# Own and receiver products of a GNN layer made in the layer itself, from stored turned rows

## The chip, the cores and the metric

The kernel runs on one core of a Trainium2 chip. The metric is the device time of one execution, in microseconds (us). The kernel before has a median of 4932.48 us over three runs (4931.5 to 4936.65).

## What is computed

Four graph layers over 12,500 nodes with 64 features each and 200,000 edges sorted by receiver. Every layer normalizes the nodes, gathers from the senders, sums into the receivers and adds to x:

```python
h = jnp.maximum(_layernorm(x, axis=-1), 0.0)
x = x + _L1_gnn_ref(h, src, dst, L1_gnn_W, L1_gnn_b)
h = jnp.maximum(_layernorm(x, axis=-1), 0.0)
x = x + _L2_gnn_ref(h, edge_attr_32, src, dst, ...)
```

Layer 1 sums the neighbours' h and multiplies. Layer 2 has a small network per edge, which is where the change is:

```python
concat = jnp.concatenate([nodes[senders], nodes[receivers], edges], axis=-1)
h = jax.nn.relu(concat @ W1 + b1)            # 160 -> 128
messages = h @ W2 + b2                       # 128 -> 64
aggregated = segment_sum(messages, receivers) / jnp.maximum(degree, 1.0)[:, None]
new_nodes = aggregated + (nodes @ Wn + bn)
```

The product of the concatenation with W1 is the sum of three: a sender part (128 wide, per node), a receiver part (128 wide, per node) and an edge part. With the own product `nodes @ Wn + bn` (64 wide), each node has 320 columns of products.

## The kernel before, in words

Nodes lie in 14 blocks of 896 (7 tiles of 128 nodes), edges in groups of 512 (4 tiles of 128). `layer_phase` (L986) builds each layer, with a program for each engine; between layers all engines meet. In the profiled execution layer 1 lies at 2203 to 2727 us of the span and layer 2 at 2731 to 4728.

Layer 1 sums most edges as dense products: 128 panel steps in each of which TensorE multiplies a piece of a table of counts with node pairs (L2356). SyncE (SP) loads the pieces, some 1575 KB each, into a ring of three (`load_piece`, L1453). VectorE adds each step's PSUM result to the accumulator (L1996 to L2000). The remaining edges come as 72 groups, whose sender rows GpSimd (POOL) gathers (L1356) four to a group into eight buffers; TensorE sums them (L2277).

As blocks of receivers are finished, their node work is laid between the panel steps, in parts 0 to 10 over seven steps: ((0), (), (1, 2, 3, 4), (), (5, 6), (7, 8), (9, 10)). Each engine's `node_part` has its share of a part; a table `parts_at` says at which step which parts of which block run. Twelve blocks run so within the panel steps and block 0 behind them; the last one, whose number is read from a table, runs at the end of the phase (`run`, L1321). For one block: ACT copies sums to `stage` (L1640), TensorE multiplies them (L2383), VectorE writes row 96 of `ht` (part 2, L2044), adds to x and normalizes (parts 2 to 4, L2033, L977 to L983, L2072), TensorE turns h in two halves (parts 5 and 7, L2395), ACT copies both to `ht`, the 97 x 896 turned rows (parts 6 and 8, L1667). In part 9 TensorE multiplies `ht` with all 320 columns of `wc2` in 7 matmuls, alternating between two PSUM tiles that ACT empties (L2408, L1682), and ACT stores the sender and receiver columns (L1686); in part 10 VectorE adds the 64 own columns to x (L2033). At the end of the phase a row block of zeros is stored behind the receiver table (L1740).

```python
for k in range(KW):
    pe.wait_ge(rows_copied, m * KW + k + (2 if k == 0 else 1))
    nc.tensor.matmul(row_ps[k % 2],
                     ht[:, k * P:(k + 1) * P], own_weights[:, :],
                     start=True, stop=True).then_inc(rows_ready, 1)
```

Layer 2 takes 392 groups. For each, POOL gathers four tiles of sender rows (L1356), SP loads edge attributes and 128 receiver rows into four slots (L1433, L1437), TensorE makes the edge part (L2257) and adds the receiver part by a selection (L2260), VectorE adds the sender rows (L1808), ACT applies the relu, and TensorE sums the messages (L2277). Into the later groups TensorE lays products of finished blocks for layer 3 (`multiply_unit`, L2372) and the node parts of layer 2's own blocks.

Of the kernel before, what the change touches and what calls it, by code (L numbers as in the profile page):

```python
# [5 lines left out]
F32 = mybir.dt.float32  # L6
# [162 lines left out]
def gnn_program(nc, x, src, dst, edge_attr, edge_type, w_rel, b_rel, w_loop, w_sum, b_sum,  # L169
# [8 lines left out]
    pair3_table = nc.dram_tensor("pair3_table", [NB, P, KW * 2 * D], F16).ap()  # L178
    counts = nc.dram_tensor("counts", [TABLE], F8).ap()
# [90 lines left out]
def setup(nc, sem, env):  # L270
# [31 lines left out]
    with ExitStack() as scope:  # L302
# [60 lines left out]
        with nc.Block() as block:  # L363
# [42 lines left out]
            def _(sp):  # L406
# [24 lines left out]
                loads.append((wc2[0:D, 0:D], env["wn_mlp"]))  # L431
                loads.append((wc2[0:D, D:D + H], env["w1_mlp"][0:D, :]))
                loads.append((wc2[0:D, D + H:], env["w1_mlp"][D:2 * D, :]))
                loads.append((wc2[D:D + 1, 0:D], bias(env["bn_mlp"])))
                loads.append((wc2[D:D + 1, D + H:], bias(env["b1_mlp"])))
# [3 lines left out]
                loads.append((wc2[DEG:DEG + 1, 0:D], bias(env["b2_mlp"])))  # L439
# [546 lines left out]
def layer_phase(nc, sem, layer, env):  # L986
# [66 lines left out]
    unit_at, unit_list = {}, []  # L1053
# [9 lines left out]
    UNIT_RING, PAIR_RING = 3, 3  # L1063

# [20 lines left out]
    if mlp:  # L1085
        unit_in = [sem(name + f"unit_in{j}") for j in range(UNIT_RING)]
        unit_ready = sem(name + "unit_ready")
        unit_low = sem(name + "unit_low")
        unit_added = sem(name + "unit_added")
        next_cleared = sem(name + "next_cleared")  # L1090
    if build:
# [61 lines left out]
    with ExitStack() as scope:  # L1153
# [7 lines left out]
        if mlp:  # L1161
            acc = sb("hidden_acc", [P, ACC_W])
            unit = [sb(f"unit{j}", [P, 4 * STRIP_COLS * KW], F8) for j in range(UNIT_RING)]
# [30 lines left out]
        if not final:  # L1194
            own_rows = DEG + 1 if nxt == 2 else D + 1
            ht = sb("ht", [own_rows, BLK])
        pair = [sb(f"pair{j}", [P, KW, 2, D], F16) for j in range(PAIR_RING if mlp else 1)] if paired else None
        rows = sb("rows", [P, KW, D + 2 * H]) if nxt == 2 else None
# [6 lines left out]
        row_ps = [ps(f"row_ps{i}")[:, 0:D + 2 * H] for i in range(2)] if nxt == 2 else None  # L1205
        out_w = D + 1 if nxt == 2 else D
        stores = 1 if final else 2
        steps = {0: 9, 1: 12, 2: 10, 3: 1}[layer]
# [136 lines left out]
        with nc.Block() as block:  # L1345
# [34 lines left out]
            def _(sp):  # L1380
# [79 lines left out]

                def load_unit(u):
                    b, n, _ = unit_list[u]
                    cols, held, _, at = PANELS[n]
# [6 lines left out]
                if dense:  # L1470
                    for s in range(max(PIECES, RING)):
                        if s < PIECES:
                            load_pairs(s)
                        if s < RING:
                            load_piece(s)
                first = sp.snap(load_first(sp))
# [76 lines left out]
            def _(act):  # L1553
# [13 lines left out]
                if nxt == 2:  # L1567
                    act.sem_inc(rows_copied, 2)

# [66 lines left out]
                def node_part(part, b, m):  # L1636
# [26 lines left out]
                    if part in (6, 8):  # L1663
                        t = (part - 6) // 2
                        w0, cols = halves[t][0] * P, len(halves[t]) * P
                        act.wait_ge(turned, m * 2 + t + 1)
                        nc.scalar.copy(ht[0:D, w0:w0 + cols], ht_ps[0:D, 0:cols]).then_inc(ht_ready, 1)  # L1667
                    if part == 8 and paired:
# [6 lines left out]
                                      pair_of(m)[:, :, :, :].rearrange("p k t f -> p k (t f)")).then_inc(stored, 16)  # L1675
                    if part == 9 and nxt == 2:
                        act.wait_ge(stored, 16 * stores * (m + 1))
                        if not isinstance(m, int) or m > 0:
                            act.wait_ge(step, m * steps)
# [3 lines left out]
                        act.wait_ge(rows_copied, (m + 1) * KW + 2)  # L1683
                        for t in range(2):
                            to = next_table[t][0:NPAD, :].rearrange("(b k p) f -> b p k f", p=P, k=KW)
                            act.dma_start(to[bass.ds(b, 1)].rearrange("a p k f -> (a p) k f"),  # L1686
                                          rows[:, :, D + t * H:D + (t + 1) * H]
                                          ).then_inc(stored, 16)
# [7 lines left out]

                if mlp:
                    def take_group(q):
# [5 lines left out]
                    for q in range(LAST_STEP):  # L1704
# [4 lines left out]
                        if q + 2 < NG:  # L1709
                            widen((q + 2) % PER)  # L1710
                        if q in parts_at:
# [25 lines left out]
                if nxt == 2:  # L1737

                    act.wait_ge(zero_ready, 1)
                    act.dma_start(next_table[1][NPAD:ACC_W, :], zero_rows[:, :]).then_inc(tail_stored, 16)  # L1740
# [20 lines left out]
            def _(dve):  # L1761
# [6 lines left out]
                if not final:  # L1768
# [252 lines left out]
                def node_part(part, b, m):  # L2021
                    xb = xs[:, bass.ds(b, 1), :].rearrange("p a (k f) -> p (a k) f", k=KW)
                    done = [{4: steps - 2, 10: steps - 1}.get(part, 0)]
# [107 lines left out]

                if mlp:
                    for q in range(3):
                        select_group(q)
                    for q in range(LAST_STEP):
# [4 lines left out]
                        if q - 1 in unit_at:  # L2140
                            add_unit(unit_at[q - 1])
                        if q + 3 < NG:
# [7 lines left out]
                        if q in parts_at:  # L2150
                            if parts_at[q][0][0] == 0:
                                dve.wait_ge(acc_added, min(q, NG) + 2)
# [343 lines left out]
```

## Time and profile before

| | us |
|---|---|
| median of three runs | 4932.48 |
| profiled execution | 4949.62 |
| span of the profiled execution | 4947.3 |
| TensorE busy | 3938.6 (80%) |
| POOL busy | 3564.0 (72%) |
| VectorE busy | 2813.5 (57%) |
| ACT busy | 2195.5 (44%) |

The span is what the profiler recorded of one execution, from the first to the last instruction; the execution's own time is 2.3 us longer. Busy shares are averages over layers that have different limits, so they say little of a change in one of them. The mean granted TensorE clock is 0.819 of its full speed; stretches with a busy TensorE show 1.00.

### The profile page before, as it was taken

Reading aid. Unit: us, or ns where it says so; the run is one execution under the profiler, and the core shown is the slowest. Engines: PE = TensorE matmul, PEld = TensorE weight load, DVE = VectorE, ACT = ScalarE, POOL = GpSimd, SP = SyncE. Lnnn points to the kernel's source line nnn. Section 1 sums busy time; section 2 is a strip of 40 time slices with the busy share of each in tenths; the row PEclk is TensorE's granted clock in tenths of the full one; section 3 lists DMA queues with packets and bytes.
Section 4 is the critical chain, followed back from the end, with each engine's and each line's share of the span. In section 5 each row is a group of like instructions: output and inputs, shape, how many; then the busy total and the mean of one; then the engine's idle time right before and its main releaser. Section 6 shows DMA issues by size and latency. Waiting matters only on the chain. (4 is left out here: it accounts for less than half of the span.)

```text
span 4947.3 us, 75766 instructions
## 1 busy us (share of the span) xinstructions
PE 3938.6 (80%) x24234; PEld 2678.4 (54%) x24249; DVE 2813.5 (57%) x7266; ACT 2195.5 (44%) x3840; POOL 3564.0 (72%) x3738
## 2 busy tenths in 40 slices
PE   6755677777788777749996688888889999999876
PEld 3354566555444443434543566666666666666643
DVE  7576999977666666643433332234445555666434
ACT  4510257767778888820111333333333333333300
POOL 6777577777777777757770677777777777777756
PEclk9855567878776778769997777789899999999888
DMA  8821223444344344448883323334445556666376
GB/s 278 325 55 36 55 89 121 132 134 130 122 133 132 120 146 132 135 117 294 279 274 119 85 80 80 80 108 130 122 133 146 157 165 170 175 170 177 98 212 175
DMA packets 580950, 719.66 MB, mean 145 GB/s; under 512 B 138104, under 2 KB 463580, under 8 KB 569952
## 3 DMA queue, kind: packets, MB, share of 16 engines
q1 hardware_dynamic: 394526, 509.02, 31.2%
q0 software_dynamic: 118064, 176.98, 14.9%
q10 hardware_dynamic: 67986, 28.96, 2.2%
q8 instruction: 199, 3.26, 0.3%
q14 instruction: 175, 1.43, 0.1%
HBM read 502.83 MB, written 217.42 MB: 146 GB/s over the span
## 5 line engine op out<-in xcount | busy, mean ns | idle before, releaser
L1356 POOL DMA_INDIRECT layer_msg<-snd_table,idx_src x1536 | 1461.3, 951 | 587.3 <-issue 458.0
L1356 POOL DMA_INDIRECT layer_msg<-rel_table,idx_rel x1440 | 1399.5, 972 | 495.2 <-issue 427.5
L1623 ACT CAST early_room<-layer_unit_ps 128x700 fp8e4<-128x700 f32 (+5 forms) x1371 | 1115.6, 884 | 483.2 <-PE layer_unit_ps L2337 368.3
L2277 PE MATMUL layer_sum_ps<-layer_sel,layer_msg 128*97 128x24 f32 (+21 forms) x6560 | 896.5, 283 | 393.1 <-DVE layer_hidden_acc L1820 150.3
L2337 PE MATMUL layer_unit_ps<-layer_hot_room,layer_low_hot 128*128 128x350 bf16 (+6 forms) x5172 | 940.9, 327 | 318.5 <-ACT early_room L1623 201.6
L2277 PEld LDWEIGHTS layer_sum_ps<-layer_sel,layer_msg 128*128 128x128 f32 (+2 forms) x6560 | 882.6, 208 | 515.5 <-issue 268.7
L2337 PEld LDWEIGHTS layer_unit_ps<-layer_hot_room,layer_low_hot 128*128 128x128 bf16 x5172 | 445.9, 124 | 732.5 <-ACT early_room L1623 550.7
L1808 DVE TENSOR_TENSOR layer_msg<-layer_pre_ps,layer_msg 128x512 f32<-128x512 f32 x392 | 270.9, 691 | 958.3 <-DMA layer_msg<-snd_table,idx_src 878.7
L1944 DVE TENSOR_SCALAR layer_hot_room<-count_iota,frame_key 128x686 bf16<-128x686 f16 (+6 forms) x2586 | 699.7, 336 | 0.0
L2260 PEld LDWEIGHTS layer_pre_ps<-layer_rcv,layer_sel_t 128*128 128x128 f32 x3144 | 476.0, 217 | 228.6 <-issue 228.6
L1356 POOL DMA_INDIRECT layer_msg<-h_table,idx_src x416 | 401.3, 965 | 181.9 <-issue 121.4
L1590 ACT COPY layer_attr_t<-layer_flip_ps 128x128 f32<-128x128 f32 x394 | 104.9, 266 | 904.0 <-PE layer_flip_ps L2249 898.6
L2356 PE MATMUL layer_panel_ps<-layer_piece,layer_pairs 128*128 128x504 fp8e4 (+3 forms) x2156 | 483.8, 378 | 20.0 <-DMA layer_piece<-counts 20.0
L2260 PE MATMUL layer_pre_ps<-layer_rcv,layer_sel_t 128*128 128x128 f32 x3144 | 471.8, 300 | 0.0
L2257 PE MATMUL layer_pre_ps<-w_edge,layer_attr_t 128*128 128x512 f32 x786 | 465.4, 678 | 0.0
L1938 DVE TENSOR_TENSOR layer_low_hot<-low_key,layer_window_iota 128x512 bf16<-128x512 bf16 x647 | 437.7, 676 | 14.3 <-PE layer_unit_ps L2337 13.7
L2372 PE MATMUL layer_unit_ps<-layer_unit,layer_pair 128*128 128x504 fp8e4 (+4 forms) x1470 | 354.9, 382 | 71.5 <-DVE acc L2019 67.9
L1600 ACT ACTIVATE layer_msg<-layer_msg 128x512 f32<-128x512 f32 x392 | 249.4, 636 | 318.4 <-DVE layer_msg L1808 317.5
L2356 PEld LDWEIGHTS layer_panel_ps<-layer_piece,layer_pairs 128*128 128x128 f16 x2156 | 206.7, 99 | 245.0 <-issue 27.7
L1820 DVE TENSOR_TENSOR acc<-acc,layer_sum_ps 64x72 f32 (+12 forms) x488 | 100.0, 205 | 353.7 <-PE layer_sum_ps L2277 341.6
L1800 DVE TENSOR_TENSOR layer_sel_bf<-rel_dst,layer_window_iota 128x512 bf16<-128x512 f32 x395 | 266.4, 675 | 4.8 <-PE layer_sum_ps L2277 2.5
L2372 PEld LDWEIGHTS layer_unit_ps<-layer_unit,layer_pair 128*128 128x128 f16 x1470 | 140.1, 99 | 209.3 <-DVE acc L2019 79.0
(290 smaller groups left out, 4028.8 us busy)
## 6 DMA issues: line engine op xcount, KB each, us to landing
counts<-early_room SPq DMA_DIRECT2D x48, 1543.5 KB
layer_unit<-counts SPq DMA_DIRECT2D x120, 441.0 KB
rel_table<-first_rows SPq DMA_DIRECT2D x98, 512.0 KB
layer_attr<-in_edge_attr_dram SPq DMA_DIRECT2D x766, 64.0 KB
layer_piece<-counts SPq DMA_DIRECT2D x24, 1575.0 KB
layer_rcv<-rcv_table SPq DMA_DIRECT2D x396, 64.0 KB
counts<-early_room SPq DMA_DIRECT2D x16, 1568.0 KB
layer_msg<-snd_table,idx_src POOLq DMA_INDIRECT x1536
```

The costliest lines, as they stand in the source:

```text
L1356: nc.gpsimd.indirect_dma_start(msg[g][:, u, 0:2 * D if dense else width], None, of, bass.IndirectOffsetOnAxis(ap=idx[:, at:at + 1], axis=0 ...
L1623: nc.scalar.copy(to[:, :, col:col + w].rearrange("p (v h) c -> p v h c", v=2), of.rearrange("p v (h c) -> p v h c", c=w), saturate=False). ...
L1800: nc.vector.tensor_tensor(to[:, :, 0:span], rel.unsqueeze(2).to_broadcast([P, TILES, span]), window_iota[:, 0:span].unsqueeze(1).to_broadc ...
L1808: nc.vector.tensor_tensor(rows_of, pre_ps[g % 2][:, :], rows_of, ALU.add).then_inc(pre_added, 1)
L1938: nc.vector.tensor_tensor(low_hot[k % HOT][:, :, :], low_key[:, at:at + TILES].unsqueeze(2).to_broadcast([P, TILES, P]), window_iota.unsqu ...
L1944: last = nc.vector.tensor_scalar(frame_hot[k % HOT][:, u, HOT_END - HI * width:HOT_END], count_iota[:, 0:HI * width], frame_key[:, at + u: ...
L2257: nc.tensor.matmul(pre_ps[g % 2][:, :], attr_t[g % 2][:, :], w_edge[:, :], start=True, stop=False)
L2260: last = nc.tensor.matmul(pre_ps[g % 2][:, u * H:(u + 1) * H], sel_t[g % 2][:, u * P:(u + 1) * P], rcv[j][:, :], start=False, stop=u == TI ...
L2277: last = nc.tensor.matmul(sum_ps[g % 2][0:rows, 0:span], msg[g][:, u, 0:rows], sel[j][:, u, 0:span], start=u == 0, stop=u == TILES - 1)
L2337: last = nc.tensor.matmul(to[:, half, :, at:at + width], low_hot[k % HOT][:, j, :], hot[:, half * HALF_ROWS * width:(half + 1) * HALF_ROWS ...
L2356: last = nc.tensor.matmul(panel_ps[k % 2][:, 0:held * cols].rearrange("p (s c) -> p s c", s=held), pairs[:, (w - ROW0) // KW, (w % KW) * 2 ...
L2372: last = nc.tensor.matmul(unit_ps[:, 0:held * cols].rearrange("p (s c) -> p s c", s=held), pair_of(b)[:, k, :, :].rearrange("p t f -> p (t ...
```

## The change

It does five things. The columns of `wc2` are put in another order (sender 0 to 127, own 128 to 191, receiver 192 to 319). In layer 1, part 9 multiplies with the 128 sender columns only, into two PSUM tiles (four and three matmuls), which ACT empties with two copies, and it stores the sender rows only. In part 8 ACT also stores the turned rows `ht`, 97 x 896 in f32, to a new table in DRAM. In layer 2, during the first 80 groups, the 14 blocks' turned rows are loaded again one by one (after group 5, 11 and so on; block 0 ahead of all), TensorE multiplies them with the other 192 columns in four pieces through the PSUM tile `unit_ps`, ACT copies each piece to SBUF and stores the receiver columns, and VectorE adds the own columns to x. The store of zeros moves to the start of layer 1.

With it come new waits. In layer 1: VectorE's part 2 and ACT's part 6 wait for the block before to have stored both its DMAs, since the next block writes the same `ht`. In layer 2: the first receiver load waits for block 0's receiver store, the load at group 92 and the first unit load for all 14; the first node part waits for all own additions.

```diff
     if part in (6, 8):            # ACT, layer 1
         act.wait_ge(turned, m * 2 + t + 1)
+        if nxt == 2:
+            act.wait_ge(stored, 16 * stores * (m + 1))
         nc.scalar.copy(ht[0:D, w0:w0 + cols], ht_ps[0:D, 0:cols]).then_inc(ht_ready, 1)
...
+    if part == 8 and nxt == 2:
+        act.wait_ge(ht_ready, m * 2 + 3)
+        act.wait_ge(x_posted, m + 1)
+        act.dma_start(env["turned_table"][bass.ds(b, 1)].rearrange("a f n -> (a f) n"), ht[:, :]
+                      ).then_inc(stored, 16)
     if part == 9 and nxt == 2:
-        for k in range(KW):
-            act.wait_ge(rows_ready, m * KW + k + 1)
-            nc.scalar.copy(rows[:, k, :], row_ps[k % 2]).then_inc(rows_copied, 1)
...
+        for t in range(2):
+            k0, n = halves[t][0], len(halves[t])
+            act.wait_ge(rows_ready, m * 2 + t + 1)
+            nc.scalar.copy(rows[:, k0:k0 + n, :], row_ps[t][:, 0:n * H].rearrange(
+                "p (k f) -> p k f", k=n)).then_inc(rows_copied, 1)
...
     if part == 2:                 # VectorE
         if nxt == 2:
-            dve.wait_ge(rows_copied, m * KW + 2)
+            dve.wait_ge(rows_copied, m * 2 + 2)
+            dve.wait_ge(stored, 16 * stores * (m + 1))
             link(nc.vector.tensor_scalar(ht[DEG:DEG + 1, :], ...
...
     if part == 10 and nxt == 2:
-        dve.wait_ge(rows_copied, (m + 1) * KW + 2)
-        add_to_x(rows[:, :, 0:D])
         dve.sem_inc(branch_begun, 1)
...
+def load_turned(b):               # SP, layer 2
+    if b:
+        sp.wait_ge(rcv_ready, RCV_PARTS * b)
+    sp.dma_start(ht[:, :], env["turned_table"][b]).then_inc(turned_in, 16)
...
     load_attr_group(q)
+    if q in (0, RCV_BY):
+        sp.wait_ge(rcv_stored, 16 * (NB if q else 1))
     load_rcv_group(q, bases[q % PER])
+    if q % RCV_EVERY == RCV_EVERY - 1 and q // RCV_EVERY + 1 < NB:
+        load_turned(q // RCV_EVERY + 1)
...
+def multiply_rcv(b):              # TensorE, layer 2
+    pe.wait_ge(turned_in, 16 * b + 16)
+    for n in range(RCV_PARTS):
+        if b or n:
+            pe.wait_ge(rcv_copied, RCV_PARTS * b + n)
+        for k in range(2 * n, min(2 * n + 2, KW)):
+            at = k % 2 * (D + H)
+            last = nc.tensor.matmul(unit_ps[:, at:at + D + H], ht[:, k * P:(k + 1) * P],
+                                    env["wc2"][:, H:], start=True, stop=True)
+        last.then_inc(rcv_ready, 1)
...
+def take_rcv(b):                  # ACT, layer 2
+    for n in range(RCV_PARTS):
+        ks = slice(2 * n, min(2 * n + 2, KW))
+        act.wait_ge(rcv_ready, RCV_PARTS * b + n + 1)
...
+        nc.scalar.copy(own_rcv[:, ks, :], ...).then_inc(rcv_copied, 1)
+    act.wait_ge(rcv_copied, RCV_PARTS * (b + 1))
+    act.dma_start(to[b], own_rcv[:, :, D:D + H]).then_inc(rcv_stored, 16)
...
+def join_own(b):                  # VectorE, layer 2
+    dve.wait_ge(rcv_copied, RCV_PARTS * (b + 1))
+    nc.vector.tensor_tensor(xb, xb, own_rcv[:, :, 0:D], ALU.add).then_inc(own_joined, 1)
```

ACT's order for one block in layer 1, before (`layer_row_ps` are the product tiles, `layer_rows` their copy):

```order
L1640 COPY layer_stage<-acc 97x896
L1658 ACTIVATE layer_rstd<-layer_rstd 128x7
L1667 COPY layer_ht<-layer_post_ps 64x512
L1667 COPY layer_ht<-layer_post_ps 64x384
L1682 COPY layer_rows<-layer_row_ps 128x320 x7
L1686 DMA snd_table<-layer_rows 128x7x128
L1686 DMA rcv_table<-layer_rows 128x7x128
```

and after the change:

```order
L1669 COPY layer_stage<-acc 97x896
L1687 ACTIVATE layer_rstd<-layer_rstd 128x7
L1698 COPY layer_ht<-layer_post_ps 64x512
L1698 COPY layer_ht<-layer_post_ps 64x384
L1710 DMA turned_table<-layer_ht 97x896
L1716 COPY layer_rows<-layer_row_ps 128x512
L1716 COPY layer_rows<-layer_row_ps 128x384
L1720 DMA snd_table<-layer_rows 128x7x128
```

Seven copies became two, and the second store moved ahead of the copies and became one of 97 rows.

SP's order in layer 2 after the change, around the second of the 14 turned loads (before, only the pairs of attribute and receiver loads stand here, `ISA` being SP's address work):

```order
L1446 DMA layer_attr<-in_edge_attr_dram 128x128
L1450 ISA
L1450 DMA layer_rcv<-rcv_table 128x128
L1477 DMA layer_ht<-turned_table 97x896
L1446 DMA layer_attr<-in_edge_attr_dram 128x128
L1450 ISA
```

A turned load stands between one group's loads and the next's, in the same queue.

TensorE's order in layer 2 after the change, around a block's products (before, L2260's receiver part was followed by L2277's sums at once):

```order
L2312 MATMUL layer_pre_ps<-w_edge,layer_attr_t 128x512
L2315 MATMUL layer_pre_ps<-layer_rcv,layer_sel_t 128x128 x4
L2491 MATMUL layer_unit_ps<-wc,layer_ht 128x192 x7
L2332 MATMUL layer_sum_ps<-layer_sel,layer_msg 128x8 x4
L2303 MATMUL layer_flip_ps<-ident_bf,layer_sel_bf 128x128 x4
```

The seven matmuls stand between one group's receiver part and the sums of the same step.

## Rows read from the trace of the kernel before

**Rows 1.** Table by windows of the core: busy us (instructions) by engine, PEclk, DMA share, GB/s.

```profile
core 0: us, PE busy (x) PEld busy (x) DVE busy (x) ACT busy (x) POOL busy (x), PEclk, DMA share, GB/s
2203.00:2640.00 437.00, 411.81 (x2192) 207.99 (x2193) 171.50 (x415) 57.93 (x122) 309.97 (x320) 0.98 0.87 284
2280.00:2400.00 120.00, 117.78 (x629) 59.90 (x627) 44.01 (x117) 19.03 (x42) 91.33 (x95) 1.00 0.86 282
2900.00:3000.00 100.00, 79.11 (x451) 61.62 (x452) 32.60 (x62) 37.62 (x80) 75.61 (x81) 0.80 0.30 79
```

**Rows 2.** Waits of POOL, 2731 to 4640 (total us, times, longest).

```profile
POOL layer_msg L1356 <- PE layer_sum_ps L2277: 9.5, 31, 0.3
```

**Rows 3.** Timeline of POOL at the last static gather (start, us, instruction, [idle before]).

```profile
2570.30 0.95 POOL L1356 DMA_INDIRECT layer_msg<-h_table,idx_src  x1 [0.30 <-issue]
```

**Rows 4.** Timeline of PE in layer 1: row multiplications and one sum.

```profile
2285.78 4.80 PE L2408 MATMUL layer_row_ps<-wc,layer_ht 97*128 97x320 f32 x14
...
2336.74 4.82 PE L2408 MATMUL layer_row_ps<-wc,layer_ht 97*128 97x320 f32 x14
...
2540.60 4.82 PE L2408 MATMUL layer_row_ps<-wc,layer_ht 97*128 97x320 f32 x14
...
2588.80 4.82 PE L2408 MATMUL layer_row_ps<-wc,layer_ht 97*128 97x320 f32 x14
...
2598.57 0.30 PE L2277 MATMUL layer_sum_ps<-layer_sel,layer_msg 128*128 128x80 f16 x4
...
2675.44 6.52 PE L2408 MATMUL layer_row_ps<-wc,layer_ht 97*128 97x320 f32 x14 [0.56 <-ACT layer_ht L1667]
```

**Rows 5.** Timeline of PE late in layer 2: receiver product of a group.

```profile
4200.03 1.05 PE L2260 MATMUL layer_pre_ps<-layer_rcv,layer_sel_t 128*128 128x128 f32 x8
```

**Rows 6.** DMA view, 4944 to 4947.3, with the issues in it.

```profile
DMA packets 882, 0.22 MB, mean 66 GB/s; under 512 B 882, under 2 KB 882, under 8 KB 882
...
out_dram<-xs ACTq DMA_DIRECT2D x1, 192.0 KB
out_dram<-xs ACTq DMA_DIRECT2D x1, 21.0 KB
```

**Rows 7.** DMA view, early copies: packets 36.3 to 40.9, one issue from 34.7.

```profile
DMA packets 468, 0.76 MB, mean 165 GB/s; under 512 B 51, under 2 KB 114, under 8 KB 468
...
acc<-acc SPq DMA_DIRECT2D x1, 31.5 KB
```

**Rows 8.** DMA view of the whole run: one issue, KB each, us to landing.

```profile
out_dram<-xs ACTq DMA_DIRECT2D x13, 224.0 KB, 3.4
```

**Rows 9.** DMA view, 2314 to 2318, while a piece streams (packets, MB, share).

```profile
DMA packets 579, 1.57 MB, mean 393 GB/s; under 512 B 60, under 2 KB 60, under 8 KB 579
...
q1 hardware_dynamic: 477, 1.45, 92.5%
```

**Rows 10.** Timeline of a block's chain, all engines, and PE's turning later.

```profile
2603.65 0.62 DVE L2044 TENSOR_SCALAR layer_ht<-acc 1x896 f32<-1x896 f32 x1
...
2610.02 0.60 PE L2395 MATMUL layer_post_ps<-ident,layer_h 128*64 128x128 f32 x4 [1.69 <-DVE layer_h L2072]
...
2613.38 2.97 PE L2356 MATMUL layer_panel_ps<-layer_piece,layer_pairs 128*128 128x512 fp8e4 x13
2613.57 0.47 ACT L1667 COPY layer_ht<-layer_post_ps 64x384 f32<-64x384 f32 x1 [2.34 <-PE layer_post_ps L2395]
...
2672.31 1.03 PE L2395 MATMUL layer_post_ps<-ident,layer_h 128*64 128x128 f32 x4 [5.84 <-DVE layer_h L2072]
```

**Rows 11.** Timeline of layer 1's end: DVE, ACT's queue, POOL, PE.

```profile
2682.46 0.68 DVE L2033 SCALAR_TENSOR_TENSOR xs<-layer_rows,ordered,xs 128x448 f32<-128x448 f32 x1 [10.30 <-ACT layer_rows L1682]
...
2724.22 0.53 ACTq L1686 DMA_DIRECT2D rcv_table<-layer_rows  x1
...
2731.64 0.94 POOL L1356 DMA_INDIRECT layer_msg<-snd_table,idx_src  x1 [119.24 <-PEq L2228]
...
2754.12 0.96 PE L2277 MATMUL layer_sum_ps<-layer_sel,layer_msg 128*128 128x8 f32 x8
```

More of the change, by code:

```diff
@@ L430, in _ @@
                 loads.append((wc1[D:D + 1, :], bias(env["b_sum"])))
[L431 to L435, printed above, removed]
+                loads.append((wc2[0:D, H:H + D], env["wn_mlp"]))
+                loads.append((wc2[0:D, 0:H], env["w1_mlp"][0:D, :]))
+                loads.append((wc2[0:D, H + D:], env["w1_mlp"][D:2 * D, :]))
+                loads.append((wc2[D:D + 1, H:H + D], bias(env["bn_mlp"])))
+                loads.append((wc2[D:D + 1, H + D:], bias(env["b1_mlp"])))
                 for u in range(TILES):
@@ L1063, in layer_phase @@
     UNIT_RING, PAIR_RING = 3, 3
+    RCV_EVERY, RCV_PARTS, RCV_BY = 6, 4, 92
+    if mlp:
+        rcv_at = {RCV_EVERY * b: b for b in range(1, NB)}
+    assert RCV_EVERY * NB < RCV_BY < BLOCK_ENDS[0]
     idx_in = [sem(name + f"idx_in{g}") for g in range(PER)]
@@ L1162, in layer_phase @@
             acc = sb("hidden_acc", [P, ACC_W])
-            unit = [sb(f"unit{j}", [P, 4 * STRIP_COLS * KW], F8) for j in range(UNIT_RING)]
+            unit_bytes = 4 * STRIP_COLS * KW
+            unit_room = sb("unit_room", [P, UNIT_RING * unit_bytes // 4])
+            unit = [unit_room[:, j * unit_bytes // 4:(j + 1) * unit_bytes // 4].bitcast(F8) for j in range(UNIT_RING)]
+            own_rcv = unit_room[:, 0:KW * (D + H)].rearrange("p (k f) -> p k f", k=KW)
         idx_slot = [sb(f"idx{g}", [P, TILES], I32) for g in range(PER)]
@@ L1204, in layer_phase @@
         unit_ps = ps("unit_ps") if mlp else None
-        row_ps = [ps(f"row_ps{i}")[:, 0:D + 2 * H] for i in range(2)] if nxt == 2 else None
+        row_ps = [ps(f"row_ps{i}") for i in range(2)] if nxt == 2 else None
         out_w = D + 1 if nxt == 2 else D
         stores = 1 if final else 2
-        steps = {0: 9, 1: 12, 2: 10, 3: 1}[layer]
+        steps = {0: 9, 1: 11, 2: 10, 3: 1}[layer]
         halves = [range(0, 4), range(4, KW)]
@@ L1695, in nodes @@
                     node_parts(range(PARTS), b, m)
+                def take_rcv(b):
+                    for n in range(RCV_PARTS):
+                        ks = slice(2 * n, min(2 * n + 2, KW))
+                        act.wait_ge(rcv_ready, RCV_PARTS * b + n + 1)
+                        if n == 0 and b:
+                            act.wait_ge(own_joined, b)
+                            act.wait_ge(rcv_stored, 16 * b)
+                        nc.scalar.copy(own_rcv[:, ks, :], unit_ps[:, 0:(ks.stop - ks.start) * (D + H)].rearrange(
+                            "p (k f) -> p k f", f=D + H)).then_inc(rcv_copied, 1)
+                    act.wait_ge(rcv_copied, RCV_PARTS * (b + 1))
+                    to = table[1][0:NPAD, :].rearrange("(b k p) f -> b p k f", p=P, k=KW)
+                    act.dma_start(to[b], own_rcv[:, :, D:D + H]).then_inc(rcv_stored, 16)
                 if mlp:
+                    take_rcv(0)
                     def take_group(q):
@@ L1767, in _ @@
                     dve.wait_ge(ht_zeroed, 1)
-                if not final:
+                if not final and not mlp:
                     nc.vector.memset(ht[D:D + 1, :], 1.0)
@@ L2022, in node_part @@
                     xb = xs[:, bass.ds(b, 1), :].rearrange("p a (k f) -> p (a k) f", k=KW)
-                    done = [{4: steps - 2, 10: steps - 1}.get(part, 0)]
+                    done = [{4: steps - (1 if nxt == 2 else 2), 10: steps - 1}.get(part, 0)]
                     def link(ins):
@@ L2404, in node_part @@
                     if part == 9 and nxt == 2:
-                        for k in range(KW):
-                            pe.wait_ge(rows_copied, m * KW + k + (2 if k == 0 else 1))
-                            nc.tensor.matmul(row_ps[k % 2],
-                                             ht[:, k * P:(k + 1) * P], own_weights[:, :],
-                                             start=True, stop=True).then_inc(rows_ready, 1)
+                        for t in range(2):
+                            pe.wait_ge(rows_copied, m * 2 + t + 1)
+                            for k in halves[t]:
+                                at = (k - halves[t][0]) * H
+                                last = nc.tensor.matmul(row_ps[t][:, at:at + H], ht[:, k * P:(k + 1) * P],
+                                                        own_weights[:, 0:H], start=True, stop=True)
+                            last.then_inc(rows_ready, 1)
                 def node_parts(parts, b, m):
```

49 lines of the change are left out of this document (34 added, 15 removed).

## Prediction, made before the changed kernel ran

> **What bounds the kernel now.** I read the table of windows first, because the change touches layer 1 (2203 to 2727 us of the span) and the start of layer 2. In layer 1 TensorE works almost without a gap: 98% busy at the full granted clock, while the DMA engines are 86% busy, mostly with panel pieces; in layer 2 TensorE is 79% busy and the DMA share is 0.30 [rows 1]. GpSimd's (POOL's) waits say what paces layer 2: its gathers waited on TensorE's sums 31 times, 0.3 us each, 9.5 us in all [rows 2], and otherwise on their own issue. A gather takes 0.95 us and 0.30 before the next [rows 3], so a group of four takes 5.0 us whatever TensorE does within it. Work added to TensorE in layer 2 lies in its idle fifth; work taken from TensorE in layer 1 can count in full, unless something there is late next. The timeline of layer 1 gives the measure: a finished block's row multiplication is 4.8 us of TensorE, and the starts of these multiplications give the block's pace [rows 4]. Seven intervals from 2336.74 to 2540.60 take 203.9 us and three from 2588.80 to 2675.44 take 86.6: ten intervals without a pause, 290.5 us, 29.05 each. Two others, 51.0 and 48.2, hold a pause.
>
> **The change part by part.**
> *Row multiplication.* Each of 7 matmuls has 128 columns instead of 320. Seven of 97x320 take 4.8 us (14 passes) [rows 4]; no row shows 97x128, so bounds: 4.8 us if columns cost nothing, and 8 passes of 128x128 in 1.05 us [rows 5], so 1.8 for 14. I take 1.8, the nearest shape: 3.0 us less per block. VectorE's wait for the seven ACT copies, 10.3 us at the last static block [rows 11], goes with its part 10. Both count only if nothing takes their place.
>
> *The store of the turned rows.* Two 448 KB stores become one of 448 KB and one of 97 rows of 3584 bytes, 347,648 bytes. The question is over how many of the 16 DMA engines these 97 rows go, and packet counts bear on it. The store of 192 KB (768 rows of 256 bytes from 128 partitions) and that of 21 KB (84 rows from 84) make 852 packets of data, and 882 are counted: 30 more, 16 + 14 [rows 6], which I read as one closing packet of each engine that takes part. Early in the run six copies, one of 31.5 KB from 63 partitions [rows 7] and five from 128, 56, 40, 1 and 1, leave 51 packets under 512 bytes: 9 + 16 + 14 + 10 + 1 + 1, each time the largest number up to 16 that divides the rows. Rounding up (63 rows in 4s, 40 in 3s) would give 16 + 16 + 14 + 14 + 1 + 1, 62. The prime 97 has no divisor from 2 to 16, so I read these counts as one engine. No row shows 97 rows themselves; the bounds are one engine and 14 (97 rows in 7s).
>
> The Trainium skill, page "DMA: Bandwidth & Descriptors", section "Why a DMA increments its semaphore by 16 and not by 1", states the same rule for the hardware queues and names 127 partitions as a case of one engine; it speaks against this change. By it the forecast below stands, and by rounding up the first rival does.
>
> *What one engine makes of it.* While a piece streams, with that queue alone at a share of 92.5%, 16 engines move 393 GB/s [rows 9], 24.6 GB/s each, so 347,648 bytes take 14.1 us on one. A piece of 1575 KB puts 4.0 us of packets on every engine. That engine shares its time with pieces: between none and all three of the piece ring stand before the store, 14.1 to 26.1 us. I take 22 (two pieces), since the share in this stage is 0.86 [rows 1].
>
> *The two new waits.* VectorE's part 2 of the next block now waits until the turned store has landed, since it writes row 96 of the same buffer, and so does ACT's copy. Queued behind VectorE's wait are its adds of panel sums and its selections, so TensorE stops for it once its PSUM tiles are full. One block's cycle then is:
> - part 2 to the end of the second copy of turned rows: 2603.65 to 2613.57 + 0.47, 10.4 us [rows 10];
> - 0.5 us of issue [rows 11], and 2.8 us from issue to landing beyond the bytes: a 224 KB store lands after 3.4 us [rows 8], of which 0.6 are bytes on 16 engines;
> - the bytes, 22 us (14.1 to 26.1);
> - the panel steps that TensorE still owes when VectorE comes free, before it can turn the new block: between none and two of 2.97 us [rows 10] at the slower pace after a wait, where four turning matmuls took 1.03 instead of 0.60 us [rows 10], so 2 x 2.97 x 1.7 = 10.1. I take 8, near that end, since the waits here are longer than that row's 5.84.
>
> Sum 43.7 us (27.8 to 49.9). Against 29.05 that is +14.65 per back-to-back block, **ten times: +146.5**. The two intervals with a pause, 51.0 and 48.2, hold 43.7: nothing (up to 49.9: +1.7). By the low end, 27.8, the wait would cost nothing either. But the engine's total work excludes that: from 2203 to 2640, 437 us, its share is 0.87 [rows 1], 380 us. Less the 11 receiver stores of 448 KB (13) and plus 12 turned stores of 14.1 (169), this engine has 536 us to do, +99; with all 284 GB/s x 437 us at the full 24.6 GB/s (315 instead of 380) it is 471, +34. The single engine thus costs 34 us at least.
>
> *Tail of layer 1.* VectorE reaches the last block's part 2 up to 10.3 us sooner [rows 11], and receiver and zero-row stores are gone from the end, where 6.9 us pass from the receiver store's issue (2724.22 + 0.53) to layer 2's first gather [rows 11]. In return the last turned store, 0.5 + 14.1 + 2.8 us, must land. I take -2 (-12 to +5).
>
> *Layer 2.* Fourteen times, every sixth group, TensorE multiplies 7 matmuls of 97x192: between 1.8 us (as 128 columns) and 4.8 (as 320). That is in 30 us of which 6 are idle [rows 1], so it is costed at nothing; were that cover gone, at most 13 x 4.8 = 62 us. ACT (38% busy) and VectorE (33%) [rows 1] take four copies of 0.5 us and one add of 0.7 per block. SP issues a turned load ahead of the next group's attribute and receiver loads: 14.1 + 2.8 = 17 us in the same queue, against four slots of 5.0 us, 20: covered, narrowly. At the start the receiver loads wait for block 0's load, products, copies and store: 2731.64 + 17.4 + 5.3 + 3.9, then 3.4 for the receiver load and about 4 of a group's work, 2766 instead of 2754.12 for the first sum [rows 11]. The gathers have eight buffers, 8 x 5.0 = 40 us from 2731.64, so until 2771.6: covered. Layer 2 gives nothing.
>
> *Sum.* 146.5 - 2 = +144.5 on the profiled execution's 4949.6 us: 5094. That execution is 17.1 us above the median of the runs, 4932.5; against the median, **5077 us**.
>
> **Rivals.**
> 1. *The store is spread* over 14 engines. Its bytes then take 1.0 us, the waits never bite, and TensorE's saving remains: the other side. For it: only that no 97-row DMA is shown. Against it: both counts [rows 6, 7]. Gain: 12 static blocks x 3.0 = 36, limited by the gathers: TensorE's last sum of the static groups, 2598.57 [rows 4], comes 27.3 us after POOL's last static gather, 2571.25 [rows 3], and cannot come closer than a group's 5.0; so 22.3 before it and 2 x 3.0 after it, 28; with the tail's -12 that is -40: 4892 us. It decides as long as the store's bytes take less than 13 us, worked out in the next rival.
> 2. *The engine's total is the bound, its wait is not*: the stores run while TensorE works on, and only the engine's 471 to 536 us count: +34 to +99, about 5000 us. For it: four of a block's seven steps lie between store and wait, 29.05 x 4/7 = 16.6 us, so 13.3 of bytes hide behind work. Against it: I expect 22.
> 3. *Layer 2 pays too*: attribute and receiver loads behind a turned load come late and TensorE uses up its slack. For it: 17 of 20 us are taken before any other traffic. Against it: a DMA share of 0.30, and 6 us in 30 to catch up. At most 13 x 5 = 65 us more; half of that, 33, and 5 at the start: 5115.
>
> **How the numbers follow.** Forecast 0.64, rival 1 0.13, rival 2 0.11, rival 3 0.12. The forecast's own ends: by the total, +34 - 2: 4965; by 49.9 us a block, +208 + 2 + 5: 5147. The range, 4965 to 5145, holds rivals 2 and 3 and leaves out rival 1 and a few hundredths beyond. A measurement of this kernel can tell 0.2%, 10 us. Faster by more is rival 1, 0.12 of its 0.13; same 0.01; slower the rest, 0.87.
>
> **What would show it.** Right: TensorE's busy share in layer 1 falls from 98 to about 70%; VectorE's part 2 waits 10 us and more on the landing of turned rows, ten times or more; row multiplications start about 44 us apart; a window that holds one turned store has one closing packet for it; layer 2 is as long as before within 15 us. Wrong: turned stores that land within 6 us and intervals of 26 us (rival 1); intervals of 33 to 38 us with short waits of VectorE (rival 2); gathers of layer 2 that wait on TensorE's sums far more than 9.5 us (rival 3).

## The result, and the profile after

The changed kernel takes 5154.3 us (median of four runs, 5151.54 to 5163.39) against 4934.35 us before: a ratio of 1.0443, interval 1.043 to 1.0456, 220 us slower. The forecast was 5077, its range 4965 to 5145: the direction is right, the size 77 us short, and the time 9 us outside the range. The profiled execution took 5153.46 us, its span is 5151.2.

To see which layer lost, I cut both spans at the first panel product of layer 1 and at the first gather of layer 2. Before, the first one is this row of TensorE's timeline (start, duration, instruction, [idle before]); the gather is in [rows 11]:

```profile
2213.65 4.92 PE L2356 MATMUL layer_panel_ps<-layer_piece,layer_pairs 128*128 128x476 fp8e4 x12 [11.84 <-DMA layer_piece<-counts]
```

After, TensorE's and POOL's timelines:

```profile
2207.52 4.00 PE L2411 MATMUL layer_panel_ps<-layer_piece,layer_pairs 128*128 128x476 fp8e4 x12 [12.05 <-DMA layer_piece<-counts]
...
2886.90 0.94 POOL L1369 DMA_INDIRECT layer_msg<-snd_table,idx_src  x1 [156.08 <-PEq L2283]
```

Layer 1 went from 2731.64 - 2213.65 = 518.0 us to 679.4, **161 us more**. The rest of the span, layers 2 and 3, went from 4947.3 - 2731.64 = 2215.7 to 2264.3, **49 us more**. The first number was forecast as 144.5, the second as nothing. (What lies ahead of layer 1 was 6 us shorter in this execution, and the profiled execution of before lay 15 us above its median: 161 + 49 - 6 = 204 between the spans, 220 between the medians. So the forecast's missing 77 us are 49 of layer 2, 17 of layer 1 and some 10 that only this difference between profiled executions and medians holds.)

*Layer 1.* The table of windows, with the columns and the first stretch of [rows 1]:

```profile
2203.00:2640.00 437.00, 305.50 (x1662) 156.67 (x1662) 123.37 (x306) 27.04 (x49) 253.42 (x266) 0.85 0.64 213
```

TensorE is busy 305.5 of 437 us, 70% instead of 94 [rows 1], at a granted clock of 0.85 instead of 0.98. VectorE's waits in layer 1 (total us, times, longest) name the cause, which did not exist before:

```profile
DVE layer_ht L2092 <- DMA snd_table<-layer_rows: 191.0, 11, 23.9
```

VectorE's and ACT's timelines show one cycle; L2092 is part 2, L1710 the turned store, L1720 the sender store:

```profile
2363.99 0.62 DVE L2092 TENSOR_SCALAR layer_ht<-acc 1x896 f32<-1x896 f32 x1 [19.54 <-DMA snd_table<-layer_rows]
...
2376.65 0.25 ACTq L1710 DMA_DIRECT2D turned_table<-layer_ht  x1
2380.77 3.96 ACTq L1720 DMA_DIRECT2D snd_table<-layer_rows  x1
2415.87 0.62 DVE L2092 TENSOR_SCALAR layer_ht<-acc 1x896 f32<-1x896 f32 x1 [21.48 <-DMA snd_table<-layer_rows]
2427.97 0.25 ACTq L1710 DMA_DIRECT2D turned_table<-layer_ht  x1
...
2461.63 0.62 DVE L2092 TENSOR_SCALAR layer_ht<-acc 1x896 f32<-1x896 f32 x1 [18.24 <-DMA snd_table<-layer_rows]
...
2836.73 0.25 ACTq L1710 DMA_DIRECT2D turned_table<-layer_ht  x1
...
2854.47 0.62 DVE L2092 TENSOR_SCALAR layer_ht<-acc 1x896 f32 x1 [2.65 <-DMA snd_table<-layer_rows]
```

Part 2 at 2363.99 is followed by the issue of the turned store 12.7 us later, at 2376.65. The next part 2 waits 21.48 us and starts at 2415.87, 39.2 us after that issue; the one after it, at 2461.63, starts 33.7 us after its store's issue. The wait's end is put down to the sender store, which VectorE's semaphore counts as well. Where no piece streams any more, at the end of layer 1, part 2 started 17.7 us after the issue (2836.73 to 2854.47). The DMA view of the first of these cycles, 2376 to 2416 (packets, MB, share of 16 engines):

```profile
DMA packets 4579, 9.70 MB, mean 242 GB/s; under 512 B 561, under 2 KB 1457, under 8 KB 4578
...
q1 hardware_dynamic: 2640, 7.92, 55.6%
q0 software_dynamic: 928, 0.95, 9.5%
q10 hardware_dynamic: 1010, 0.81, 5.9%
...
layer_piece<-counts SPq DMA_DIRECT2D x3, 1575.0 KB
layer_piece<-counts SPq DMA_DIRECT2D x1, 1562.5 KB
layer_piece<-counts SPq DMA_DIRECT2D x1, 1449.0 KB
...
snd_table<-layer_rows ACTq DMA_DIRECT2D x1, 448.0 KB
turned_table<-layer_ht ACTq DMA_DIRECT2D x1, 339.5 KB
```

The ACT queue has 1010 packets: 97 turned rows, 896 sender rows, and 17 more, 16 for the sender store's engines and **one** for the turned store's. In these 40 us five pieces were issued. The 7.92 MB of pieces that moved are 20.1 us of each engine at 24.6 GB/s, the gathers' 9.5% are 3.8, the sender rows 1.2, and on the one engine 14.1 more: 39.2 us. By this estimate that engine had next to no pause, while the mean share of all 16 was 71%.

*Layer 2.* SP's, TensorE's and POOL's timelines around the second turned load (L1477; L1446 are attribute loads, L2332 TensorE's sums):

```profile
2925.23 0.96 PE L2332 MATMUL layer_sum_ps<-layer_sel,layer_msg 128*128 128x8 f32 x8
...
2925.95 0.32 SPq L1477 DMA_DIRECT2D layer_ht<-turned_table  x1
2926.31 0.40 SPq L1446 DMA_DIRECT2D layer_attr<-in_edge_attr_dram  x1
...
2928.14 0.96 PE L2332 MATMUL layer_sum_ps<-layer_sel,layer_msg 128*128 128x8 f32 x8
...
2933.93 0.96 PE L2332 MATMUL layer_sum_ps<-layer_sel,layer_msg 128*128 128x8 f32 x8
2944.18 0.58 PE L2303 MATMUL layer_flip_ps<-ident_bf,layer_sel_bf 128*128 128x128 bf16 x4 [9.29 <-issue]
...
2949.20 0.94 POOL L1369 DMA_INDIRECT layer_msg<-snd_table,idx_src  x1 [2.67 <-PE layer_sum_ps L2332]
```

The attribute load issued behind the turned load belongs to a group that TensorE could begin after its sums of 2933.93; it begins at 2944.18 after 9.29 us idle, 18 us after the turned load's issue. There are thirteen such stretches, one behind each turned load from the second on. The profile names no releaser for them; that it is the attribute load follows from the order here, and from e3 and e10 below, where such idle time is under 1 us in all. POOL then waits for a buffer. TensorE's idle time of this kind in layer 2, and POOL's waits on TensorE's sums, against 9.5 us in [rows 2]:

```profile
PE layer_flip_ps L2303 <- issue: 93.7, 13, 9.3
```

```profile
POOL layer_msg L1369 <- PE layer_sum_ps L2332: 66.7, 41, 3.0
```

### The profile page after: what moved, and what is told of

The parts are those of the page before. It is cut to its first block and busy times, and to the rows that moved or that the text cites. A ratio compares the mean times of both kernels' runs of the same rounds, so it can differ in the third digit from the quotient of the medians.

```text
span 5151.2 us, 76229 instructions
## 1 busy us (share of the span) xinstructions
PE 3924.5 (76%) x24430; PEld 2680.8 (52%) x24445; DVE 2816.3 (55%) x7265; ACT 2186.0 (42%) x3826; POOL 3553.0 (69%) x3738
## 3 DMA queue, kind: packets, MB, share of 16 engines
q0 software_dynamic: 118064, 176.98, 14.3%
## 5 line engine op out<-in xcount | busy, mean ns | idle before, releaser
L2332 PE MATMUL layer_sum_ps<-layer_sel,layer_msg 128*97 128x24 f32 (+21 forms) x6560 | 890.1, 282 | 301.9 <-DMA layer_msg<-rel_table,idx_rel 129.2
L2332 PEld LDWEIGHTS layer_sum_ps<-layer_sel,layer_msg 128*128 128x128 f32 (+2 forms) x6560 | 884.4, 208 | 410.7 <-issue 241.7
L2315 PEld LDWEIGHTS layer_pre_ps<-layer_rcv,layer_sel_t 128*128 128x128 f32 x3144 | 455.8, 209 | 220.2 <-issue 220.2
L2411 PE MATMUL layer_panel_ps<-layer_piece,layer_pairs 128*128 128x504 fp8e4 (+3 forms) x2156 | 507.8, 391 | 43.7 <-DMA layer_piece<-counts 42.1
L2312 PE MATMUL layer_pre_ps<-w_edge,layer_attr_t 128*128 128x512 f32 x786 | 453.6, 662 | 0.0
L2315 PE MATMUL layer_pre_ps<-layer_rcv,layer_sel_t 128*128 128x128 f32 x3144 | 451.6, 291 | 0.0
L1985 DVE TENSOR_TENSOR layer_low_hot<-low_key,layer_window_iota 128x512 bf16<-128x512 bf16 x647 | 438.2, 677 | 10.4 <-PE layer_unit_ps L2392 9.8
L2429 PE MATMUL layer_unit_ps<-layer_unit_room,layer_pair 128*128 128x504 fp8e4 (+4 forms) x1470 | 346.7, 375 | 80.7 <-DVE acc L2066 78.2
L2429 PEld LDWEIGHTS layer_unit_ps<-layer_unit_room,layer_pair 128*128 128x128 f16 x1470 | 136.8, 98 | 217.6 <-DVE acc L2066 94.1
```

The costliest lines, as they stand in the source:

```text
L1985: nc.vector.tensor_tensor(low_hot[k % HOT][:, :, :], low_key[:, at:at + TILES].unsqueeze(2).to_broadcast([P, TILES, P]), window_iota.unsqu ...
L2312: nc.tensor.matmul(pre_ps[g % 2][:, :], attr_t[g % 2][:, :], w_edge[:, :], start=True, stop=False)
L2315: last = nc.tensor.matmul(pre_ps[g % 2][:, u * H:(u + 1) * H], sel_t[g % 2][:, u * P:(u + 1) * P], rcv[j][:, :], start=False, stop=u == TI ...
L2332: last = nc.tensor.matmul(sum_ps[g % 2][0:rows, 0:span], msg[g][:, u, 0:rows], sel[j][:, u, 0:span], start=u == 0, stop=u == TILES - 1)
L2411: last = nc.tensor.matmul(panel_ps[k % 2][:, 0:held * cols].rearrange("p (s c) -> p s c", s=held), pairs[:, (w - ROW0) // KW, (w % KW) * 2 ...
L2429: last = nc.tensor.matmul(unit_ps[:, 0:held * cols].rearrange("p (s c) -> p s c", s=held), pair_of(b)[:, k, :, :].rearrange("p t f -> p (t ...
```

## The experiments

The theory: a transfer of 97 rows runs on one of the 16 engines; in layer 1 VectorE waits for it behind the pieces, and in layer 2 small loads queue behind it. All kernels are compared with the kernel before on the same chip. "Layer 1" and "rest" are cut as above.

| run | what differs from the changed kernel | median us | ratio to before, interval | layer 1 | rest |
|---|---|---|---|---|---|
| kernel before | | 4934 to 4946 | | 518.0 | 2215.7 |
| changed kernel | | 5154.3 | 1.0443, 1.043 to 1.0456 | 679.4 | 2264.3 |
| e1_both_112 | 112 rows | 4900.13 | 0.9916, 0.9899 to 0.9932 | 474.7 | 2212.0 |
| e2_store_112 | store 112, load 97 | 4956.43 | 1.0028, 1.0017 to 1.0039 | 475.5 | 2265.1 |
| e3_load_96 | store 97, load 96 + 1 | 5105.83 | 1.0324, 1.0306 to 1.0341 | 686.1 | 2212.8 |
| e4_two_ht | two buffers | 5014.28 | 1.0143, 1.0126 to 1.016 | 538.1 | 2264.1 |
| e5_both_100 | 100 rows | 4900.03 | 0.9917, 0.9901 to 0.9934 | 472.2 | 2213.3 |
| e6_both_101 | 101 rows | 5203.25 | 1.0531, 1.0514 to 1.0549 | 690.2 | 2300.6 |
| e7_rows_64_1 | rows 0 to 63 and 96 alone | 4897.61 | 0.9911, 0.9895 to 0.9928 | 475.2 | 2211.4 |
| e8_own_wait | wait for the turned store alone | 5094.66 | 1.0309, 1.0292 to 1.0326 | 612.5 | 2270.4 |
| e9_half_rows | as e8, rows in two halves | 5182.11 | 1.0479, 1.0462 to 1.0497 | 654.3 | 2309.7 |
| e10_load_act | turned loads on ACT's queue | 5117.48 | 1.0349, 1.0332 to 1.0366 | 678.7 | 2221.6 |

**More engines: e1, e2, e3.** The edit of e1 adds rows of zeros (`TURNED` is 112; these are two of its lines); e2 loads only 97 of the 112, e3 splits the load alone:

```diff
-    turned_table = nc.dram_tensor("turned_table", [NB, DEG + 1, BLK], F32).ap()
+    turned_table = nc.dram_tensor("turned_table", [NB, TURNED, BLK], F32).ap()
-            ht = sb("ht", [own_rows, BLK])
+            ht = sb("ht", [TURNED if nxt == 2 or mlp else own_rows, BLK])
```

> The turned rows get 112 instead of 97 rows (15 rows of zeros more, 15% more bytes), in the store and in the load; every wait stays. One-engine theory: 112 is 16 x 7, so all 16 engines share each transfer, the store lands in some 6 us instead of 39, the next block's part 2 no longer waits, and block intervals in layer 1 return to some 26 us; layer 1 (first panel product to layer 2's first gather, 518 us before, 679 with the change) takes 478 to 490, layer 2 and 3 (2216 before, 2264 with the change) 2216 again: some 4892 to 4905 us. Rival, the wait itself (a store behind streaming pieces is slow on any number of engines): layer 1 stays above 640 us, 5110 us or more.

> As the run before, but layer 2 loads 97 of the 112 rows. One-engine theory: layer 1 as in the run before (478 to 490 us), layer 2 and 3 keep the 49 us that they gained, since the load still goes over one engine: 4941 to 4955 us. Rival, layer 2's loss has nothing to do with how the load is spread (it is TensorE's added products and the late start): no difference to the run before by this edit, both keep the 49 us.

> The store of the changed kernel, 97 rows; the load of layer 2 is split into 96 rows and one row. One-engine theory: layer 1 stays at 679 us, layer 2 and 3 fall back to 2216 to 2226: some 5105 to 5115 us. Rival (layer 2's loss is the products or the late start): no change, 5154.

With 112 rows layer 1 falls to 474.7 us, 43 below the kernel before, and the rest to 2212.0. The window of layer 1 is back at 92% busy and the clock at 0.98:

```profile
2203.00:2640.00 437.00, 401.33 (x2290) 211.46 (x2290) 169.35 (x418) 40.09 (x73) 306.95 (x319) 0.98 0.87 287
```

VectorE's wait is down to 1.5 us:

```profile
DVE layer_ht L2093 <- DMA snd_table<-layer_rows: 1.5, 2, 0.8
```

e2 has e1's layer 1 and the changed kernel's rest; e3 the reverse. The time of e2 (1 us above) and layer 1 of both (3 us below) lie just outside the ranges of the theory, and far from the rivals'. So the two losses are separate: the store's one engine is worth 679.4 - 475 = 204 us of layer 1, the load's 52 us of layer 2. The products that layer 2 took over cost nothing that can be seen: e1 has them too.

**Which row counts: e5, e6.** Only `TURNED` changes.

> The turned rows have 100 rows, three of zeros more than the changed kernel. If the number of engines is the largest one up to 16 that divides the rows, 100 rows go over 10 engines, 1.5 us of bytes at 24.6 GB/s each, and the kernel is as fast as with 112 rows: 4900 us, layer 1 475 to 482 us. Rival (what 112 rows cure is something else, such as a multiple of 16 rows): as slow as with 97, 5154.

> One row of zeros more than the run before: 101 is prime. If the divisor decides, store and load go over one engine again, with 4% more bytes than 97 rows: layer 1 near 679 us plus 5 to 15, layer 2 and 3 near 2264, in all 5154 to 5175 us. Rival (rounding up: 101 rows in 7s over 15 engines): 4900 us.

The ACT queue's packets in a window that holds one turned and one sender store, for 112, 100 and 101 rows:

```profile
q10 hardware_dynamic: 1040, 0.86, 14.0%
```

```profile
q10 hardware_dynamic: 1022, 0.82, 9.7%
```

```profile
q10 hardware_dynamic: 1014, 0.82, 5.9%
```

Less 896 + 16 of the sender store, 128, 110 and 102 are left: 112 + 16, 100 + 10, 101 + 1. So 100 rows take 10 engines and cost as little as 112, and one row more costs 303 us. That settles the divisor. Layer 1 of e6 is 11 us longer than with 97 rows, as expected; its rest is 36 us longer, where I expected no change. The excess is again POOL's wait on TensorE's sums, 101.0 us in layer 2 instead of 66.7; why 4% more bytes cost so much there stays open.

**Wait or engine: e4.** Turned rows and sender rows get two buffers each, with a semaphore for each:

```diff
-                            dve.wait_ge(stored, 16 * stores * (m + 1))
+                            free(dve, m)
```

`free` waits for the two stores of the block before the last one only, and ACT's copies use it too.

> The 97-row store and load stay on one engine, but the turned rows and the sender rows have two buffers each in layer 1, so that a block waits for the stores of the block before the last one only. If the latency of one store is what costs (forecast), layer 1 falls until the one engine's total work is the bound: 34 to 99 us above the 518 of before instead of 161, so 5027 to 5092 us. Rival (the engine's total work is the bound already): no change, 5154, and VectorE's waits stay as long as they were in all (191 us).

```profile
PE layer_panel_ps L2433 <- DMA layer_piece<-counts: 41.1, 16, 12.0
...
DVE layer_ht_odd L2113 <- DMA snd_table<-layer_rows: 3.2, 1, 3.2
```

VectorE's wait for stores shrinks from 191 us to 3.2, and layer 1 is 20 us longer than before instead of 161. So the wait cost 141 us. What remains is the loaded engine. The 20 us lie below my 34 to 99, because the expectation left out what this kernel saves elsewhere in layer 1, 43 us by e1: with these, the engine's work costs 538.1 - 474.7 = 63 us, inside the bounds. Of these, 27 are TensorE's longer wait for pieces (41.1 us against 14.3 in e1; the changed kernel has 34.3), and 19 its panel products, which take 371.3 us in all against 352.0, at a granted clock of 0.94 against 0.99 from 2213 to 2640. The rest was not followed further.

**Which store the wait is for: e8.** The turned store gets its own semaphore, which VectorE's part 2 and ACT's copies wait for; the wait for the sender store moves to part 9, ahead of the copies that write its buffer:

```diff
-                            dve.wait_ge(stored, 16 * stores * (m + 1))
+                            dve.wait_ge(turned_out, 16 * (m + 1))
```

> 97 rows, one buffer, one engine as in the changed kernel; but the next block waits for the turned store alone, no longer for the sender store issued 4.3 us after it on the same queue. If the turned store's own 39 us on the shared engine are the wait, this gives back only the sender store's part on that engine: 1.2 us of bytes, 2.4 us when shared with pieces, 12 times, 14 to 29 us: 5125 to 5140. Rival (the wait ends with the sender store, which is late by itself, by its later issue and landing, 6 us or more per block): 72 us less or more, 5080 or lower.

```profile
2457.28 0.25 ACTq L1713 DMA_DIRECT2D turned_table<-layer_ht  x1
2461.39 3.75 ACTq L1724 DMA_DIRECT2D snd_table<-layer_rows  x1
2486.06 0.62 DVE L2099 TENSOR_SCALAR layer_ht<-acc 1x896 f32<-1x896 f32 x1 [16.40 <-DMA turned_table<-layer_ht]
2498.48 0.25 ACTq L1713 DMA_DIRECT2D turned_table<-layer_ht  x1
...
2523.87 0.62 DVE L2099 TENSOR_SCALAR layer_ht<-acc 1x896 f32<-1x896 f32 x1 [10.33 <-DMA turned_table<-layer_ht]
```

Layer 1 falls by 67 us, near the rival's 72 and far from my 14 to 29 (the whole by 60: the rest grew by 6). Part 2 now starts 28.8 and 25.4 us after the turned store's issue in the two cycles shown, 25.4 to 30.8 in eight and 34.9 in one with a pause, where in the changed kernel it started 31.9 to 39.2. The sender store, though 1.2 us of bytes on that engine, held the next block some 8 us longer: it stands behind the turned rows in the same queue. The changed kernel's own trace shows its part there. From the last turned row to shortly before the wait's end, 2453.4 to 2461.2, the ACT queue moves 57 packets, 56 sender rows and one closing packet, in 7.8 us; at the end of layer 1, where no piece streams, 2852.25 to 2853.7 holds the last turned row's closing packet and the same 57 in 1.4 us:

```profile
q10 hardware_dynamic: 57, 0.03, 1.2%
```

```profile
q10 hardware_dynamic: 58, 0.03, 6.6%
```

The rows follow each other there every 0.14 us and every 0.024 us: the difference is about one packet of a piece (3.0 KB, 0.12 us at 24.6 GB/s).

**How the engine is shared: e9.** On e8's base, the rows leave in 194 packets instead of 97:

```diff
-                        act.dma_start(env["turned_table"][bass.ds(b, 1)].rearrange("a f n -> (a f) n"), ht[:, :]
+                        act.dma_start(env["turned_table"][bass.ds(b, 1)].rearrange("a s f n -> (a f) s n"),
+                                      ht[:, :].rearrange("f (s n) -> f s n", s=2)
```

> On the run with its own wait for the turned store: the same bytes of turned rows in 194 runs of 1792 bytes instead of 97 of 3584, still on one engine. Theory of turns: that engine serves the two queues packet by packet, so each turned packet waits for one piece packet of 3.0 KB (0.12 us): 97 x (0.146 + 0.122) = 26 us, which the 25 to 26 us from issue to wait's end agree with; halves make 194 x (0.073 + 0.122) = 38 us, 12 us more in some ten blocks, layer 1 612 + 100 to 130, the whole some 5195 to 5225 us. Rival (the queues share the engine by bytes, or the store is served behind whole pieces): no change in layer 1 beyond 15 us, 5095 to 5110.

```profile
q10 hardware_dynamic: 1107, 0.81, 6.0%
```

The packets are 194 + 896 + 1 + 16 = 1107. Layer 1 grows by 42 us: more than sharing by bytes allows, about a third of what a turn at every packet would cost; part 2 starts 31 to 38 us after the issue in nine cycles, 26.5 in one. The DMA view shows the pace where the ACT queue moves turned rows alone: in the changed kernel from 2391.5 to 2406.5, in e9 from 2390.5 to 2406, and in e9 from 2788 to 2794, where no piece streams:

```profile
q10 hardware_dynamic: 55, 0.20, 3.2%
```

```profile
q10 hardware_dynamic: 81, 0.15, 2.4%
```

```profile
q10 hardware_dynamic: 75, 0.13, 6.5%
```

So a row took 0.27 us beside pieces, a half row 0.19, and a half row alone 0.08: again one piece packet more. The Trainium skill, page "DMA: Bandwidth & Descriptors", section "Queues, rings and completion order", says that an engine goes round between its queues packet by packet, typically with some 9 to 17 descriptors to a packet. The trace agrees that it goes round; a turn here was a single row or half row. What the expectation had wrong is that every packet meets a turn. By the starts of the single packets, of a transfer beside pieces 64 to 79 of 96 gaps between turned rows hold a turn (over 0.08 us beyond the row's own time) in the changed kernel, and 71 to 145 of 193 in e9; in the others the next row follows at its own pace. Why those hold none is not shown.

**Layer 2's queue: e10.** ACT issues the turned loads, each behind the receiver store of the block before:

```diff
...
+                    if b + 1 < NB:
+                        act.dma_start(ht[:, :], env["turned_table"][b + 1]).then_inc(turned_in, 16)
```

> The changed kernel, but ACT issues layer 2's turned loads on its own queue, each right behind the receiver store of the block before, so attribute and receiver loads no longer queue behind them. Still 97 rows on one engine. Theory (the 49 us of layer 2 are loads that queue behind a turned load in SP's queue): layer 2 and 3 fall from 2264 to 2213 to 2225, in all 5105 to 5115 us. Rival (it is the shared engine, whatever the queue): 2250 to 2264, 5140 to 5154.

```profile
POOL layer_msg L1369 <- PE layer_sum_ps L2326: 9.4, 18, 4.2
```

The rest falls from 2264.3 to 2221.6, as expected (the whole, 5117.48, lies 2 us above its range), and POOL's waits from 66.7 to 9.4 us, with the same 97 rows on one engine. The load itself is covered; what cost 43 of the 49 us is that the small loads stood behind it in SP's queue (the load's time of issue moved with the queue; the two were not taken apart).

**The best version: e7.** Only rows that carry data are stored and loaded:

```diff
+                        act.dma_start(to[0:D, :], ht[0:D, :]).then_inc(stored, 16)
+                        act.dma_start(to[D:D + 1, :], ht[DEG:DEG + 1, :]).then_inc(stored, 16)
```

> Only the rows that carry data are stored and loaded: 64 rows of h (16 engines) and the row of degrees (one row on one engine, 3584 bytes, 0.15 us); the rows of ones and zeros are set once in layer 2. 233 KB per block instead of 401. One-engine theory: as with 112 rows, 4895 to 4902 us, since there VectorE waited for stores 1.5 us in all and nothing is left to gain. Rival (the bytes, 12 x 170 KB in a stage with 86% DMA share, still cost): 5 to 10 us below the run with 112 rows.

4897.61 us against 4940.41, 0.9911 of before: 43 us faster. It can't be told from e1 or e5, so with the stores spread, their bytes cost nothing that can be measured. All three beat both kernels.

## Why the prediction was wrong

*What held.* The mechanism is the one forecast: 97 rows on one engine (e1, e5, e6), VectorE's part 2 waiting for the landing, TensorE's share at 70%, nine waits of over 10 us where ten or more were named, one closing packet. The time from issue to part 2 with nothing beside the store, 17.7 us against 0.5 + 2.8 + 14.1 = 17.4, came out by offsetting errors: the sender store is in it with 1.4 us, and what is not bytes was 1 to 2 us, not 3.3. Behind pieces it was 25.4 us and more (e8), forecast 0.5 + 2.8 + 22 = 25.3. The first rival's price was right in sum: 4892 us for a spread store, e1 measured 4900, 42 us below the kernel before on its chip, where 40 were forecast. Its parts were off in opposite directions: the twelve intervals between row multiplications gave 25 us (forecast 28), the tail 18 (forecast 12).

*The step that failed, layer 2: "covered, narrowly. Layer 2 gives nothing."* The 17 us of the load were right (18 seen). The cover of four slots of 5.0 us was not: when TensorE is behind it takes a group in 2.9 us (its sums at 2925.23 and 2928.14 above), so four slots last some 12 us, and an idle stretch like the 9.29 us follows the load. This was rival 3, priced at 38 us and given 0.12; it measured 49, beside the forecast rather than in its place. Without it the kernel would have taken 5106 us (e3), inside the range.

*The step mis-sized, layer 1's cycle of 43.7 us.* Seven of the ten intervals between turned stores measured 44.6 to 47.6 us, two 50.5 and 51.3, and the last, with few pieces left, 26.7: 452 us, forecast 437 (from part 2 at 2415.87: 12.1 us to the issue at 2427.97, then 33.7 to the next part 2, 45.8). Two terms were wrong in opposite directions. "The panel steps that TensorE still owes", 8 us, hardly exist: 12 to 13 us pass from part 2 to the issue, against 10.4 without them, so some 2. In their place stands the sender store, some 8 us (e8): the sum has the landing of the turned store alone, though the semaphore counts both. By the packets of the cycle from 2427.97 the 33.7 us are 0.8 to the first turned row, 24.6 for the rows (forecast 22), 7.8 for the sender rows and 0.5 to part 2; so what is not bytes took 1.3 us, where 3.3 were forecast, and the bytes took turns with pieces rather than standing behind two of them. That the sum came within 4 us of seven of the ten intervals is thus in part luck. The two intervals with a pause, put at nothing, grew to 55.7 and 52.4 us, 9 more. The ten intervals' 15 us and these 9 are 24; the two ends of layer 1 came out some 7 below the forecast, 4 of them in the tail (from the last of these row multiplications to layer 2's first gather 56.2 us before, 2836.76 to 2886.90 or 50.1 after: -6, where -2 was forecast), and 17 are left between 161.4 and 144.5.

*Rival 2* fell: with the wait gone (e4) the loaded engine alone costs 63 us against e1, but in the changed kernel the wait decides.

## What to carry to other kernels

Before a transfer is added, look at its row count: a count with no divisor from 2 to 16 (97 and 101 here) puts all of it on one engine, which showed as one closing packet, and padding, splitting or leaving rows out is free by comparison (303 us between 100 and 101 rows). A semaphore that counts two stores makes the waiter pay for the later one, even when only the first protects its buffer. And a long load ahead of small ones in the same queue needs a cover that is counted in the consumer's own pace after a stall, not in the mean pace; another queue gave most of it back.

## What the runs showed that I had not expected

One row of zeros more than 97 + 3 costs 303 us; and against 97 rows, 101 cost 36 us in layers 2 and 3 (2300.6 against 2264.3), far more than 4% of bytes, in e9 194 smaller packets 39 us (2309.7 against 2270.4). Both show as POOL's wait on TensorE's sums in layer 2 (101.0 us against 66.7, and 109.5 against 70.4 in e8); why a slightly later load costs so much there, no run here tells. A sender store that has 1.2 us of bytes on the shared engine delayed its waiter by 8 us, since its rows there took turns with piece packets. TensorE's lower clock cost something too: its panel products of layer 1 took 375.4 us in all in the changed kernel, at a granted clock of 0.85 from 2213 to 2640, and 352.0 in e1, at 0.99.
